# Windowed attention of a vision tower on one core: each step's values product moved one step later, its normalising product moved from VectorE to GpSimd, the interleaved products spread anew

## The reference

```
# second layer: windowed attention with four experts, 12 heads of 16, causal within 64 tokens
for e in range(4):
    q, k, v = (x @ w.T for w in (wq[e], wk[e], wv[e]))       # 512 x 192 each, split into 12 heads of 16
    scores  = where(mask, q @ k.T * 16 ** -0.5, NEG)           # per image and head, 64 x 64
    o       = softmax(scores) @ v
    outs.append(o @ wo[e].T)
fused = concat(outs)                                         # 512 x 768
h = layernorm(h + silu(fused @ w_gate.T) * (fused @ w_up.T))
```

## Time and profile before

| | us |
|---|---|
| median of 3 runs | 411.57 (411.3 to 412.5) |
| profiled execution, its own time | 411.31 |
| its span in the trace | 409.6 |
| around the span (start and end of the execution) | 1.7 |
| TensorE busy | 384.5 (94% of the span) |
| VectorE busy | 250.9 (61%) |
| ScalarE busy | 174.7 (43%) |
| GpSimd busy | 45.6 (11%) |
| the second attention's 16 steps, up to the last join | 114.92 to 206.06 |

### The profile page before, as it was taken

The page is one execution under the profiler, slowest core; times in us unless marked ns, Lnnn a source line. Parts: engine busy times, 40 slices in busy tenths (PEclk is TensorE's granted clock), DMA queues, the critical chain, the costliest instruction groups (busy, mean ns, idle before and its releaser), DMA issues.

```text
span 409.6 us, 8771 instructions
## 1 busy us (share of the span) xinstructions
PE 384.5 (94%) x3602; PEld 315.0 (77%) x3602; DVE 250.9 (61%) x728; ACT 174.7 (43%) x304; POOL 45.6 (11%) x97
## 2 busy tenths in 40 slices
PE   8999999999877899999999989999999999999993
PEld 8988878788554657565548788998999899879783
DVE  1567766603497988888444487558458206677344
ACT  1256551842455565755435635235224310551420
POOL 7130010330000000100001400000000200304003
PEclk9999999999978999999999999999999989989999
DMA  7999500000289100000003996224401000000001
GB/s 194 258 223 252 118 9 2 2 0 0 61 229 272 53 2 2 2 2 3 2 0 87 280 265 162 77 60 134 130 9 56 2 0 2 2 2 2 0 2 38
DMA packets 28725, 30.69 MB, mean 75 GB/s; under 512 B 4867, under 2 KB 24137, under 8 KB 28686
## 3 DMA queue, kind: packets, MB, share of 16 engines
q1 hardware_dynamic: 28220, 29.96, 29.1%
q10 hardware_dynamic: 306, 0.17, 0.2%
q0 software_dynamic: 160, 0.01, 0.0%
HBM read 29.73 MB, written 0.39 MB: 74 GB/s over the span
## 4 chain that ended last, share of the span: by engine, by line
PE 73%; DVE 15%; ACT 5%; issue 2%; DMA 2%; POOL 2%; SPq 0%; DVEq 0%; POOLq 0%
PE ps L1510 66%; PE ps L1514 6%; DMA front<-in_x 2%; DVE front L1170 2%; DVE front L1171 2%; PE ps L1522 2%; DVE front L1179 1%; DVE front L1181 1%; DVE front L1164 1%; DVE bn L1015 1%; POOL rstd L524 1%; ACT front L745 1%; DVE front L1166 1%; DVE xn L1030 1%; DVE mv L1018 0%
## 5 line engine op out<-in xcount | busy, mean ns | idle before, releaser
L1510 PE MATMUL ps<-halves 128*128 128x512 f32 (+2 forms) x380 | 84.1, 376 | 1.3 <-ACT front L732 1.3
L1510 PEld LDWEIGHTS ps<-halves 128*128 128x128 f32 x380 | 66.5, 188 | 13.4 <-ACT front L732 1.7
L1510 PE MATMUL ps<-wide,front 128*128 128x192 f32 x432 | 73.7, 332 | 0.0
L1510 PEld LDWEIGHTS ps<-wide,front 128*128 128x128 f32 x432 | 72.0, 194 | 1.0 <-issue 0.5
L1510 PEld LDWEIGHTS ps<-front 64*32 64x32 f32 (+3 forms) x1488 | 52.0, 134 | 21.8 <-issue 9.4
L1510 PE MATMUL ps<-front 64*32 64x64 f32 (+3 forms) x1488 | 60.7, 245 | 8.1 <-ACT front L745 3.0
L732 ACT ACTIVATE front<-ps,colc 128x512 f32<-128x512 f32 x60 | 39.6, 690 | 52.3 <-PE ps L1510 52.2
L1313 DVE SCALAR_TENSOR_TENSOR xn<-ps,small,xn 128x192 f32<-128x192 f32 x28 | 9.7, 410 | 29.7 <-PE ps L1510 29.7
L1514 PE MATMUL ps<-ident,front 128*128 128x128 f32 x144 | 21.5, 286 | 6.5 <-DVE front L1181 5.3
L1514 PEld LDWEIGHTS ps<-ident,front 128*128 128x128 f32 x144 | 16.2, 144 | 10.2 <-DVE front L1181 7.2
L1510 PE MATMUL ps<-xT,turned 128*64 128x256 f32 (+1 forms) x96 | 23.4, 482 | 0.0
(11 more groups left out here) (280 smaller groups left out, 555.5 us busy)
## 6 DMA issues: line engine op xcount, KB each, us to landing
wide<-in_w SPq DMA_DIRECT2D x8, 576.0 KB, 4.7
wide<-in_w SPq DMA_DIRECT2D x8, 384.0 KB, 5.8
wide<-in_w SPq DMA_DIRECT2D x16, 192.0 KB, 6.3
front<-in_a2w SPq DMA_DIRECT2D x5, 576.0 KB
front<-in_a1w SPq DMA_DIRECT2D x5, 384.0 KB
front<-in_x SPq DMA_DIRECT2D x3, 512.0 KB, 7.9
front<-in_w_qkv SPq DMA_DIRECT2D x2, 576.0 KB, 7.7
front<-in_a1w SPq DMA_DIRECT2D x5, 192.0 KB
```

Source lines behind the costliest of these rows:

```text
L1510: return pe.matmul(o, l, r, start=start, stop=stop)
```

## The change

TensorE's `values1(n)` goes one step later, so that a step is: scores of n + 2, the extra, transposes of n, values of n - 1. The normalising product moves from VectorE to GpSimd: VectorE leaves its reciprocals in a new small buffer `sum1` (two of them) and counts `sum1_done`, GpSimd multiplies and counts `p1_done`. The extras are given to other steps, and at the start the scores of step 1 change places with the second half of the first values. ScalarE's list follows: an extra's first copy, `exp1(n + 2)`, `pT1_out(n)`, an extra's second copy, `fade_out`, `oT_out(n - 1)`, `fT_out`. GpSimd's cut of the decay table stands between its products 10 and 11.

```diff
         mx1 = take(2, 2 * PAIRS)
+        sum1 = take(2, 2 * PAIRS)
...
+            for n in range(EA * NT):
+                if n == 11:
+                    decay_cut()
+                pk = p1[:, n % 3].rearrange("p a m j -> p (a m) j")
+                pool.wait_ge(s["sum1_done"], n + 1)
+                pool.tensor_tensor(pk, pk, sum1[:, n % 2, :].unsqueeze(2).to_broadcast([P, 2 * PAIRS, S]),
+                                   ALU.mult).then_inc(s["p1_done"], 1)
             norm()
...
             for n in range(N1):
                 e, t = divmod(n, NT)
-                pT1_out(n)
-                if e < EA - 1:
-                    if t == 0 and e >= 1:
-                        qk_out(e + 1, 0)
-                    elif t == 1:
-                        qk_out(e + 1, 2)
-                    elif t == 3:
-                        v_out(e + 1, 0)
+                if t == 0 and e < EA - 1:
+                    qk_out(e + 1, 2)
+                elif e == 0 and t == 1 or e == 1 and t == 2:
+                    v_out(e + 1, 0)
+                elif e == EA - 2 and t >= 2:
+                    v_out(e + 1, t - 2)
+                elif e == 0 and t >= 2:
+                    qk_out(2, t - 2)
+                elif e == 1 and t == 3:
+                    qk_out(3, 0)
                 if n + 2 < N1:
                     exp1(n + 2)
+                pT1_out(n)
+                if e == 0 and t == 1 or e == 1 and t == 2:
+                    v_out(e + 1, 1)
+                elif e == 1 and t == 3:
+                    qk_out(3, 1)
                 if 4 <= n < 4 + PAIRS:
                     fade_out(n - 4)
-                if e < EA - 1:
-                    if t == 0 and e >= 1:
-                        qk_out(e + 1, 1)
-                    elif t == 3:
-                        v_out(e + 1, 1)
-                if e >= 1 and t == (2 if e < EA - 1 else 0):
+                if n >= 1:
+                    oT_out(n - 1)
+                if e >= 1 and t == 1:
                     fT_out(e - 1)
-                oT_out(n)
                 if e == EA - 1 and t >= 2:
 
                     act.wait_ge(s["v1_mm"], 2 * EA)
                     w1_high(t - 2)
+            oT_out(N1 - 1)
             fT_out(EA - 1)
...
                 dve.wait_ge(s["exp1"], n + 1)
-                link(dve.tensor_reduce(mx1[:, x, :], pk, AX.X, ALU.add))
-                link(dve.reciprocal(mx1[:, x, :], mx1[:, x, :]))
-                dve.tensor_tensor(pk, pk, mx1[:, x, :].unsqueeze(2).to_broadcast([P, 2 * PAIRS, S]),
-                                  ALU.mult).then_inc(s["p1_done"], 1)
+                if n >= 2:
+                    dve.wait_ge(s["p1_done"], n - 1)
+                link(dve.tensor_reduce(sum1[:, x, :], pk, AX.X, ALU.add))
+                dve.reciprocal(sum1[:, x, :], sum1[:, x, :]).then_inc(s["sum1_done"], 1)
...
             scores1(0)
             values_in(0, 0)
+            scores1(1)
             values_in(0, 1)
-            scores1(1)
             project1(1, 1)
             project1(1, 0)
...
                 if n + 2 < N1:
                     scores1(n + 2)
-                turn1(n)
-                if e < EA - 1:
...
-                values1(n)
-
-            gate_up(1, first)
+                if t == 0 and e < EA - 1:
+                    project1(e + 1, 2)
+                elif e == 0 and t == 1 or e == 1 and t == 2:
+                    values_in(e + 1, 0)
+                    values_in(e + 1, 1)
+                elif e == 0:
+                    project1(2, t - 2)
+                elif t == 1:
+                    join(e - 1, 0)
+                    join(e - 1, 1)
+                elif e == 1:
+                    project1(3, 0)
+                    project1(3, 1)
+                elif e == EA - 2:
+                    values_in(e + 1, t - 2)
+                elif t == 2:
+                    pe.wait_ge(s["fT_top"], EA - 1)
+                    pe.wait_ge(s["fT_end"], EA - 1)
+                    gate_up(2, first)
+                    gate_up(3, first)
+                elif t == 3:
+                    pe.wait_ge(s["s1_read"], N1)
+                    gate_up(0, first)
+                    gate_up(1, first)
+                turn1(n)
+                if n >= 1:
+                    values1(n - 1)
+            values1(N1 - 1)
             join(EA - 1, 0)
             join(EA - 1, 1)
```

More of the change, by code:

```diff
@@ L296, in vit_tower @@
             mixer_left h_mm h_act y_mm y_half y_done
-            qk1_mm qk1_done v1_mm v1_done s1_mm s1_read sub1 exp1 t1_mm pT1_done pv1_mm p1_done
+            qk1_mm qk1_done v1_mm v1_done s1_mm s1_read sub1 exp1 t1_mm pT1_done pv1_mm sum1_done p1_done
             oT1_done wo1_mm fT_top fT_end gu_mm silu_done
@@ L550, in _, with decay_cut @@
             tell(pool.memset(vz, 0.0), "zeros_made")
[L552 to L559, removed]
+            def decay_cut():
+                pool.wait_ge(s["decay_exp"], 1)
+                for h in range(2):
+                    r = slice(64 * h, 64 * h + 64)
+                    ins = pool.affine_select(out=decay[r, 0:PAIRS], in_=decay[r, 0:PAIRS], compare_op=ALU.is_ge, fill=0.0, base=0,
+                                             pattern=[[0, PAIRS], [1, S]], channel_multiplier=-1)
+                    if h == 0:
+                        link(ins)
+                tell(ins, "decay_done")
+            for n in range(EA * NT):
[5 more added lines that the diff above has]
+                                   ALU.mult).then_inc(s["p1_done"], 1)
             norm()
@@ L1989, in _ @@
                     scores1(n + 2)
-                turn1(n)
-                if e < EA - 1:
[L1992 to L2003, removed]
+                if t == 0 and e < EA - 1:
[6 more added lines that the diff above has]
+                elif t == 1:
                     join(e - 1, 0)
                     join(e - 1, 1)
-                elif t < 3:
+                elif e == 1:
[4 more added lines that the diff above has]
+                elif t == 2:
                     pe.wait_ge(s["fT_top"], EA - 1)
                     pe.wait_ge(s["fT_end"], EA - 1)
-                    gate_up(t + 1, first)
-                else:
+                    gate_up(2, first)
+                    gate_up(3, first)
+                elif t == 3:
                     pe.wait_ge(s["s1_read"], N1)
                     gate_up(0, first)
-                values1(n)
-            gate_up(1, first)
+                    gate_up(1, first)
[3 more added lines that the diff above has]
+            values1(N1 - 1)
             join(EA - 1, 0)
```

## The result

The changed kernel takes 415.28 us (median of 20 executions, 409.95 to 417.49), the kernel before 411.69 (20 executions, 409.63 to 414.34). The ratio of the means is 1.006, with a 95% interval of 1.003 to 1.009: slower by 0.6%, where 411.3 us and no change were forecast. Five of the 20 executions, those above 416.1 us, count as slow and are left out of this ratio, so that it is smaller than the 3.6 us between the medians. The profiled execution is one of the long ones, 416.6 us with a span of 414.9.

What follows compares the result with a forecast made beforehand. TensorE's work, 78.2 of the stage's 91.14 us, was taken as fixed. Old waits and lost clock 12.9 against new waits 13.1 gave 411.7; another count won 0.8; the middle, 411.3, was forecast, range 410.1 to 412.5.

Steps and rivals of the forecast that it cites:

- TensorE's waits in the new order: Section laying the engines' lists side by side, scores of step 2 to last join: TensorE's new waits together 13.1 us.
- The old order's slow stretch: Seven microseconds from 118.4 at granted clock 0.51: 2.7 us lost, of which only 1.6 showed because waits hid part.
- What bounds the kernel now: Opening section on the 91.14 us stage: 12.9 us can be won, the other 78.2 are TensorE's work at full clock.
- Waits and lost clock, 12.9 us, are all that a new order can win: Old order's stage: TensorE idling 10.2 us plus 2.7 us of lost clock, the most any new order can win.
- The slow stretch should be gone: After 116 to 118.4, where TensorE idled twice, the new order idles only 0.4 us, so the clock should hold.
- the sum: Whole stage: old waits and lost clock 12.9 us against new waits 13.1, so +0.2 us, giving 411.7.
- differs by 0.8 us: Second count, bookkeeping of both orders at full clock side by side: the change wins 0.8 us rather than losing 0.2.
- lower end of 1.7: Estimated shortest time of GpSimd's 768-column product, from its additions; 1.9 us taken, upper end 2.4, outer end 2.8.
- rival 2: GpSimd's product takes long, 2.4 to 2.8 us: +1.2 to +3.8, so 412.6 to 415; chance 0.15.
- 3: Clock falls again, in steps 11 to 13 after 3.1 us of idling: 2.7 to 3.4 us, 414 to 415; chance 0.12.
- Rival 4: ScalarE's queue shorter than laid out, waits of joins and fT_out (7.1 us) halve: 407.8; chance 0.21 with small gains.
- Rivals 1: VectorE's masks also wait for GpSimd's product, round 6.2 us, VectorE sets every step: +8, some 419; chance 0.10.

Runs made afterwards that it cites:

- before_load: The kernel before with SyncE's loads of the next layer's weights held until five values products are done: 411.07 us, the kernel before 411.22.
- fill_end: The changed kernel with five dummy TensorE products ahead of the last join: 412.25 us, against 412.50 for the changed kernel.
- ot_first: The changed kernel with ScalarE's last output copy put ahead of w1_high(1): 412.35 us, 0.15 under the changed kernel.
- load_late: The changed kernel with SyncE's loads of the next layer's weights held until five values products are done: 412.40 us, the kernel before 412.12.
- ft_early: The changed kernel with ScalarE's copies of a join (fT_out) ahead of the transposes' copy: 409.34 us, ratio to the kernel before 0.993.
- the combos: The changed kernel with ft_early's and ot_first's edits and gate_up(1) back ahead of values(15): 407.22 us; with eight dummies added 408.36; further edits: combo2.
- combo2: The first of the combos, with the output copies that joins need put ahead and the loads held: 403.96 us, ratio to the kernel before 0.981.

## Why the prediction was wrong

**What held.** "TensorE's waits in the new order" came out nearly wait by wait, apart from those of steps 2, 4 and 11 (below). Before project1(1, 2) 0.49 for 0.4; join(0) and join(1) 1.25 each for 1.1 and 1.5; values_in(2) and (3) 0.92 and 1.06 for 1.05 each; the gates 1.55 for 1.7; values(15) 0.59 for 0.6; the last join 0.93 for 1.2; transposes 12 2.16 for 2.4. The old order's slow stretch cost its stage 1.7 us (91.14 for the 89.46 of before_load), for the 1.6 worked out. The Trainium skill's rule (SBUF — State Buffer, "Who interferes with whom"), by which the mask is free of GpSimd's port, is borne out by 32 masks at 417 ns beside 16 products; for the subtraction these runs can't test it, since the product was always over.

**The step that failed** is in "What bounds the kernel now": "the other 78.2 us are TensorE's work at full clock, and the change leaves every product in place". That put at nothing all that a new order does to TensorE beside its waits for other engines. At full clock these are the 2.0 us by which the stage is longer: a stop within values(1), 1.35 us in that trace and 0.7 to 1.35 in eight, and 0.8 us of longer busy time (78.99 for 78.15). The stop was in neither sum nor rivals, and the trace before shows none. Of the busy time I can only say that the joins hold 0.3 of it; what makes them longer stays open.

**A second step failed beside it:** "Waits and lost clock, 12.9 us, are all that a new order can win", with "The slow stretch should be gone". It took the 2.7 us that the clock cost in one execution for a property of the old order, and let it pay for 2.9 us more of waits (13.1 for 10.2). The trace of before_load is the old order with no slow stretch, and the new order has slow places of its own in step 12 and at the last join. Both orders should have been compared at full clock.

**Luck in the sum.** At full clock the waits are even, 11.3 before and 11.1 after, and the sum had them nearly even, 12.9 and 13.1. But the first held 1.6 us of clock that can't be credited, and the second was 2.0 us too long; the two errors cancelled. The other count in the text, "differs by 0.8 us", doesn't agree with its own terms: 10.2 and the 1.1 us of waits that the slow stretch hid make 11.3, and 13.1 less 11.3 is 1.8, not 0.8. I took the middle of two counts of one thing without asking why they were 1.0 apart. Left at 0.8 us against the change, the forecast would have been 412.4, nearer to what came, but for longer waits that aren't there.

**What was mis-sized.** The product: 1.9 taken, 1.47 measured, under my lower end of 1.7. With 0.22 us for the start, 1.47 leaves 1.6 ns a column, where 1.9 had been taken from the additions; whether the broadcast, the multiplication or the length makes it cheaper, no run separates. The product takes 1.5 times VectorE's 0.96, where rival 2 had about twice. The shorter product made the waits of steps 2, 4, 11 and 12 shorter (0.15, 0, 0 and 2.16, for 0.55, 0.4, 0.35 and 2.4), 1.4 us of the 13.1. In the two traces with a slow step 12 join(2) didn't wait at all, for 0.7; in the trace at full clock it waited 0.80.

**Of the rivals,** 3 is the one that came nearest: the clock fell behind the wait of step 12, as it said, and gave a time of 415. But it was described as a risk of the new order alone, where every order has slow stretches in some executions. Whether the idling makes them stays open. The two kernels with dummies didn't gain, but neither filled the 2.16 us ahead of transposes 12. Six traces have that wait whole, and in five of them the clock falls at its end or just behind it (changed kernel twice, fill_end, ot_first, load_late); in the four traces of ft_early and the combos, where it is 1.57 or filled, step 12 runs at full clock. That points at the wait but doesn't show it, since the old order of before_load has a wait of 1.98 and no fall. Dummies in the 2.16 us of the changed kernel are the run that is missing. Rival 4's mechanism (ScalarE's queue shorter than laid out) was refuted; that its order was the lever is what ft_early and combo2 showed. Rivals 1 and 2 did not occur.

## What to carry to other kernels

Compare two orders at the same clock, and never credit a change with a slow stretch that one profiled execution happened to have: look at several executions, each with its granted clock, and compare times at equal clock. When a stage passes from one bound to another, the next thing late is often not an engine's work but its order: ScalarE was busy 49 of 92 us and still made TensorE wait 7.5, and putting what the next product needs ahead of what is needed a step later made the kernel 0.8 us faster than before at equal clock with `fT_out` alone (2.8 between the medians) and 7.2 us with the other moves and the held loads, where the change by itself lost 1.8. Moving a product to a slower engine paid only together with an order that covers its longer path; each half alone lost, 3.0 and 5.5 us at equal clock (4.3 and 10.2 between the medians). And a new order of TensorE's list can cost time with every wait as forecast: leave room for it in the range.

## What the runs showed of the hardware

- A GpSimd product of 128x768 with a broadcast operand takes 1.47 us, 1.92 ns a column with its start, where four additions of 192 columns, none broadcast, took 2.24: here the same number of columns in one instruction was a third cheaper.
- TensorE stopped for 0.7 to 1.35 us inside an unbroken group of products, waiting for no engine, at the same product in eight traces, while loads ran at about 200 to 380 GB/s. With the loads held back the stop was gone, and with the products in the old order it didn't come in spite of the loads. Two stops of one trace lie 126 or 751 products apart, with as many weight loads.
- The spread of this kernel from one execution to the next, 409 to 417 us, follows the mean granted clock, with correlations of -0.89 to -0.91 in the three groups of 25 to 29 executions, at 2.3 to 2.9 us per 0.01 of clock.
